# Kept rows of a routed FFN: gathered by index on GpSimd and turned on TensorE, in place of products with a choice matrix

## What is computed

```python
def ffn(x, w_r, b_r, w1, b1, w2, b2):        # x: attention's output, 64 x 64 x 512
    k = int(l * 0.5)                         # 32 of the 64 tokens of a sequence
    scores = jnp.einsum('bld,d->bl', x, w_r) + b_r
    _, idx = jax.lax.top_k(scores, k)
    x_sel = jnp.take_along_axis(x, idx[:, :, None], axis=1)
    h = jax.nn.gelu(jnp.einsum('bkd,df->bkf', x_sel, w1) + b1)
    out_sel = jnp.einsum('bkf,fd->bkd', h, w2) + b2
    return jnp.zeros_like(x).at[batch_ix, idx].set(out_sel)
```

## Time and profile before

| | |
|---|---|
| time, median of 3 runs | 2159.59 us (2158.35 to 2160.52) |
| the profiled execution: time, span | 2162.24 us, 2160.4 us |
| PE busy over the span | 1944.0 us, 90% |
| DVE, ACT, POOL busy | 72%, 56%, 55% |
| granted TensorE clock, mean | 0.966 |
| L1589 (products with `keep`) from 1300 to 1960 us | 23.2 us busy, x168 |

### The profile page before, as it was taken

One profiled execution on the slowest core, in us unless ns is written; L12 is line 12 of the kernel. 1 busy time (PEld: TensorE's weight loads), 2 busy tenths in 40 slices (PEclk: granted clock), 3 DMA queues, 4 the chain that ended last, 5 costly groups with the idle time before them and its releaser, 6 DMA issues.

```text
span 2160.4 us, 33041 instructions
## 1 busy us (share of the span) xinstructions
PE 1944.0 (90%) x9664; PEld 1344.5 (62%) x9664; DVE 1547.9 (72%) x2697; ACT 1199.8 (56%) x3210; POOL 1196.5 (55%) x1162
## 2 busy tenths in 40 slices
PE   5789998999899899978569999999999999999999
PEld 4666666676667666655246766757566575665755
DVE  6799999999999999999257654545545454554412
ACT  2666676666666666655246654645546454554512
POOL 1477887788877888777577763443443434340000
PEclk8899999999999999999879999999999999999999
DMA  4421332333323332230377443333233323331011
GB/s 141 168 110 66 129 118 90 115 129 129 121 83 121 129 120 107 88 113 30 101 208 246 134 115 96 83 102 104 80 109 93 102 76 96 95 85 37 14 52 47
DMA packets 149546, 225.83 MB, mean 105 GB/s; under 512 B 49859, under 2 KB 109254, under 8 KB 144002
## 3 DMA queue, kind: packets, MB, share of 16 engines
q1 hardware_dynamic: 116306, 161.94, 21.9%
q0 software_dynamic: 31744, 61.07, 10.1%
q10 hardware_dynamic: 1328, 0.91, 0.1%
HBM read 211.44 MB, written 40.51 MB: 117 GB/s over the span
## 4 chain that ended last, share of the span: by engine, by line
PE 43%; issue 2%; POOL 2%; DMA 2%; DVE 1%; ACT 1%; DVEq 0%; POOLq 0%; ACTq 0%
PE attn_psum L1610 11%; PE attn_psum L1624 10%; PE attn_psum L1576 5%; PE attn_psum L1562 4%; PE attn_psum L1549 4%; PE attn_psum L1542 4%; PE attn_psum L1533 2%; PE attn_psum L1640 2%; PE attn_psum L1589 1%; DMA kv<-in_kv_rows,old_now 1%; POOL kv L1214 1%; POOL kv L1206 1%; PE attn_psum L1523 1%; DMA kv<-kv_scratch,new_now 0%; ACT xh L1295 0%
## 5 line engine op out<-in xcount | busy, mean ns | idle before, releaser
L417 POOL TENSOR_TENSOR hid<-hid,bc 128x1024 f32<-128x1024 f32 x256 | 620.6, 2434 | 192.9 <-DVE hid L810 192.3
L938 PE MATMUL scan_psum<-hid,ident 128*128 128x256 f32 x2048 | 540.1, 394 | 108.9 <-POOL hid L417 108.9
L810 DVE TENSOR_TENSOR_SCAN hid<-scan_psum,dbu 128x1024 f32<-128x1024 f32 x256 | 581.7, 2273 | 4.7 <-ACT scan_psum L460 4.6
L938 PEld LDWEIGHTS scan_psum<-hid,ident 128*128 128x128 f32 x2048 | 383.9, 194 | 286.6 <-POOL hid L417 143.8
L460 ACT ACTIVATE scan_psum<-delta,neg_a 128x252 f32<-128x252 f32 x1024 | 423.9, 465 | 122.9 <-DVE hid L810 120.9
L1402 DVE CUSTOM_DVE_ANT_0 prob<-attn_psum,mask 128x336 f32<-128x336 f32 x256 | 120.6, 505 | 384.5 <-PE attn_psum L1542 383.0
L754 DVE TENSOR_TENSOR dbu<-scan_psum,bc 128x1024 f32<-128x1024 f32 x256 | 307.2, 1200 | 0.1
L1263 ACT COPY p_t<-attn_psum 112x384 f32<-112x384 f32 x256 | 121.5, 483 | 293.1 <-PE attn_psum L1549 292.8
L903 PE MATMUL scan_psum<-w_qkv,x 128*128 128x512 f32 x512 | 260.2, 594 | 3.9 <-ACT sq L520 2.4
L1624 PE MATMUL attn_psum<-w,ffn_hid 128*128 128x512 f32 x512 | 239.0, 596 | 8.9 <-DVE y_sb L1454 8.9
L1610 PE MATMUL attn_psum<-xs_in,w 128*128 128x256 f32 x1024 | 238.0, 387 | 0.6 <-ACT th L1296 0.5
(11 more groups left out here) (176 smaller groups left out, 2619.4 us busy)
## 6 DMA issues: line engine op xcount, KB each, us to landing
bc<-bc_scratch SPq DMA_DIRECT2D x32, 2048.0 KB, 7.3
q_scratch<-qg SPq DMA_DIRECT2D x32, 260.0 KB, 2.1
q_in<-q_scratch SPq DMA_DIRECT2D x32, 260.0 KB
x_pair<-in_x_pairs SPq DMA_DIRECT2D x32, 256.0 KB, 2.8
xt<-in_x_tp SPq DMA_DIRECT2D x16, 512.0 KB, 8.4
x_scratch<-x SPq DMA_DIRECT2D x16, 512.0 KB, 2.9
kv_scratch<-kvg SPq DMA_DIRECT2D x32, 256.0 KB, 2.0
w<-in_w SPq DMA_DIRECT2D x8, 1024.0 KB, 9.1
```

Source lines behind the costliest of these rows:

```text
L417: pool.tensor_tensor(hid[:, r, :, :], hid[:, r, :, :], bc[q // 2][:, 4 * j:4 * j + 4, 1, :], ALU.mult).then_inc(pool_hc, 1)
L810: nc.vector.tensor_tensor_scan(hid[:, k % RING, :, :].rearrange("p n t -> p (n t)"), decay[k % 2], dbu[:, k % RING, :, :].rearrange("p n t ...
L938: mm = nc.tensor.matmul(yc, ident[:], hid[:, k % RING, i, :], start=False, stop=(k % 4 == 3 and i == 3))
```

## The change

- **Rows by index.** `router_take`, `take_rows`, the store of `xs` and `load_xs` go. SP stores each pair's `a_sb` to memory as it is (`store_a`, 256 KB a pair). POOL gathers the 128 kept rows of two pairs with one indirect DMA (`gather_rows`) to `x_rows`, 128 by 512, PE turns them in four transposes (`turn_x`) into `a_bank`, and ACT copies them to `xs_in` (`take_x`): for tt = 0 in pair 4(t+1)+1 and for tt = 1 in pair 4(t+1)+2, both in w = 0. In the latter `ffn_first` stands two items later in PE's queue and waits for `take_x`.
- **Scores spread by a turn.** `router_row` is one transpose of the scores, each repeated along a row; `r_diag` goes.
- **Ranks spread by a turn.** `router_keep` is cut in two. `router_rank` (the counting) moves to the head of DVE's w = 3, before the two maxima. PE turns the ranks (`router_ranks`) in w = 3 between its two `turn_p`. `router_keep`, at its old place, waits for that and makes `keep_t` with one comparison, then the index list `r_idx` with two more instructions.
- **POOL's loop.** The second eight sequences are written out too, so the loop runs from 2. A gather of tile t's rows stands behind sequence 8(t+1)+5 for tt = 0 and behind sequence 8(t+2)+1 for tt = 1.

```diff
-            for s in range(NKV):
-                gather(0, s)
-            with pool.Fori(1, B // NKV) as i:
+            def gather_rows(t, tt):
+                wait(pool, dve_keep, 2 * (4 * t + 2 * tt + 2), pool_mark)
+                for h in range(2):
+                    wait(pool, st_a[h], 16 * (2 * t + tt + 1), pool_mark)
+                wait(pool, pe_xt, 2 * t + tt - 1, pool_mark)
+                pool.indirect_dma_start(x_rows[tt][:], None, S["a"][tt],
+                                        bass.IndirectOffsetOnAxis(ap=r_idx[tt][:, 0:1], axis=0)
+                                        ).then_inc(ld_xg[tt], 16)
+            def eight(i):
                 for s in range(NKV):
                     gather(i, s)
+                    if s == 5:
+                        gather_rows(i - 1, 0)
+                    if s == 1 and not (isinstance(i, int) and i == 1):
+                        gather_rows(i - 2, 1)
...
+            eight(1)
+            with pool.Fori(2, B // NKV) as i:
+                eight(i)
...
+            def take_x(t, tt):
+                act.wait_ge(pe_xt, 2 * t + tt + 1)
+                wait(act, pe_h, NH * t)
+                nc.scalar.copy(xs_in[:, :, P * tt:P * tt + P], a_bank.rearrange("p (c t) -> p c t", c=NCH)
+                               ).then_inc(act_xt, 1)
...
+            def router_keep(m, i, j):
+                h = j % 2
+                rows = slice(64 * h, 64 * h + 64)
+                dve.wait_ge(pe_rank, m + 1)
+                wait(dve, st_keep[h], 16 * (2 * i + j // 2))
+                v.scalar_tensor_tensor(keep_t[h][rows, :], a_bank[rows, P:2 * P], slot_no[rows, :], slot_own[rows, :],
+                                       ALU.is_equal, ALU.mult).then_inc(dve_keep, 1)
...
-                nc.tensor.matmul(a_bank[:, 0:P], ones[:], r_diag[:], start=True, stop=True).then_inc(pe_row, 1)
+                nc.tensor.transpose(a_bank[:, 0:P], r_s[:].to_broadcast([P, P]), ident[:]).then_inc(pe_row, 1)
-            def router_take(m, h):
-                pe.wait_ge(dve_keep, m + 1)
-                nc.tensor.matmul(a_bank[64 * h:64 * h + 64, P:2 * P], keep[:], ident[:], start=True, stop=True)
+            def router_ranks(m):
+                pe.wait_ge(dve_rank, m + 1)
+                nc.tensor.transpose(a_bank[:, P:2 * P], r_rank[:].to_broadcast([P, P]), ident[:]).then_inc(pe_rank, 1)
+            def turn_x(t, tt, m):
+                pe.wait_ge(ld_xg[tt], 16 * (t + 1))
+                wait(pe, act_xt, 2 * t + tt)
+                wait(pe, dve_keep, 2 * min(m - 1, NG) if isinstance(m, int) else 2 * (m - 1))
                 for c in range(NCH):
-                    mm = nc.tensor.matmul(a_bank[:, 2 * P + 2 * SEL * c:2 * P + 2 * SEL * c + 2 * SEL],
-                                          a_sb[:, P * c:P * c + P], keep[:], start=True, stop=True)
-                mm.then_inc(pe_xs, 1)
+                    mm = nc.tensor.transpose(a_bank[:, P * c:P * c + P], x_rows[tt][:, P * c:P * c + P], ident[:])
+                mm.then_inc(pe_xt, 1)
...
-                    pe.wait_ge(ld_xs, 16 * (t + 1))
+                    pe.wait_ge(act_xt, 2 * (t + 1))
...
-                    if w == 0 and parts.prev2:
-                        router_take(m - 2, h)
+                    if w == 0 and parts.first and j in (1, 2):
+                        turn_x(i - 1, j - 1, m)
...
+                    if w == 3 and parts.prev:
+                        router_ranks(m - 1)
```

More of the change, by code:

```diff
@@ L1009, in attention_ffn_block @@
         r_s = sb("r_s", [P, 1])
-        r_diag = sb("r_diag", [P, P])
+        r_tok = sb("r_tok", [P, 1])
+        r_idx = [sb(f"r_idx{i}", [P, 1], I32) for i in range(2)]
         r_own, r_gt, r_eq, r_rank = (sb(n, [P, 1]) for n in ("r_own", "r_gt", "r_eq", "r_rank"))
-        keep = sb("keep", [P, 2 * SEL])
         keep_t = [sb(f"keep_t{i}", [P, P]) for i in range(2)]
-        xs = [sb(f"xs{i}", [P, NCH, 2 * SEL]) for i in range(2)]
+        x_rows = [sb(f"x_rows{i}", [P, D]) for i in range(2)]
         w1, w2 = W["w1"], W["w2"]
@@ L1167, in pair @@
                 if parts.prev2:
-                    store_rows(m - 2, 2 * i + j // 2 - 1, h)
-                if parts.first and j == 1:
-                    load_xs(i - 1)
+                    store_keep(m - 2, 2 * i + j // 2 - 1, h)
+                if parts.prev:
+                    store_a(m - 1, i if j else i - 1, (j - 1) % 4)
                 if parts.second and j < 2:
@@ L1573, in project @@
                 pe.wait_ge(act_o, m + 1)
-                wait(pe, act_xs, 2 * m)
+                wait(pe, dve_keep, 2 * m)
+                if turned is not None:
+                    pe.wait_ge(act_xt, turned)
                 for c in range(4):
@@ L1704, in program @@
     S["keep"] = nc.dram_tensor("keep_scratch", [NG, 2 * SEL, P], F32).ap()
[L1705 to L1706 removed]
+    S["a"] = [nc.dram_tensor(f"a_scratch{i}", [2 * P, D], F32).ap() for i in range(2)]
     with ExitStack() as ctx:
```

103 lines of the change are left out of this document (55 added, 48 removed).

## The result

The changed kernel takes 2201.3 us (median of 5 runs, 2193.39 to 2204.69), the kernel before 2160.52 beside it (2158.35 to 2163.7): ratio 1.0185, 95% interval 1.017 to 1.0199. It is slower by 41 us where 4.8 were forecast. Its profiled execution took 2193.39 us (span 2191.6) and was its fastest; its other four show a lower mean clock (0.949 to 0.953 against 0.957) with their longer spans.

The account below looks back on a forecast made before the run. PE was taken to bound the kernel from pair 6 on. Start wait 17.1, clock 2.5, slots -28.6 and DVE wait 13.4, plus 0.4, gave +4.8 us: 2164.4 against the median 2159.59, range 2152 to 2177.

Parts of the forecast that it names:

- The start wait: First FFN product, pair 6: waits for tile 0's second row gather in POOL's queue, starting at 1224.7 not 1207.56, +17.1 us.
- The bound of 23: Upper end, in us, of the start-wait term, if POOL's written-out sequences are no faster than its loop.
- The clock behind it: After PE's idle time in pair 6: granted clock falls, costing 2.5 us, ends 1.7 and 3.4.
- The saved slots: PE from pair 6 on: choice and score products go, turns come, -28.6 us.
- The wait of DVE: DVE waits for PE's turned ranks, so everything behind the maxima is 0.57 us late: +13.4 us, ends 5 and 20.
- Place (1): A tile's second pair: PE's wait for take_y grows from 1.36 to 1.95 us, six times, +3.5; pair 33 adds 1.1.
- R: Start of PE's rank turn, near the end of each pair; the forecast counts DVE's chain of instructions from it.
- Place (2): A tile's third pair: PE waits 1.3 us for take_x behind ACT's two exponentials, six times, 7.8; pair 34 adds 0.9.
- Place (3): A tile's last pair and the next tile's first: a GELU product stands between, so PE waits only 0 to 0.1 us.
- rival D: Clock falls at the new PE waits of some 2.0 us, twelve falls of 2.2 each: 2191 us; chance 0.08.
- 0.4 added for rounding: Added to the summed terms, +4.4 us, for place (3) and for issue costs that rows round away, giving +4.8.
- A: The terms hold as summed: 2164.4 us, ends 2158 to 2172; chance 0.64.

## Why the prediction was wrong

It had the sign and rivals that name most of what happened, and a time 37 us too low: outside its range. Term by term, against the two profiled executions:

**The start wait: right in mechanism and place, 3.9 short.** Forecast 1224.7 for the first FFN product, found 1228.55, +21.0. The step that failed is that eight written-out sequences would go at the 8.0 us of four earlier ones. POOL opens sequence 8 at 1136.05 and sequence 16 at 1206.07, with one gather of rows in between, so 8.6 each. Six of the eight took 7.9 to 8.4, but sequence 8 took 11.5, since one issue in it stood for 3.41 us for a landing. Rows 4 had a sign of this: sequences 6 and 7, written out as well, took from 1118.37 to 1136.27, 8.95 each, with a stand of 2.14 for a landing. What holds such landings up no run shows. The first row is of the kernel before, the two behind it are of the changed kernel:

```profile
1124.72 0.98 POOL L1214 DMA_INDIRECT kv<-kv_scratch,new_now  x1 [2.14 <-DMA kv<-in_kv_rows,old_now]
...
1143.97 0.99 POOL L1216 DMA_INDIRECT kv<-kv_scratch,new_now  x1 [3.41 <-DMA kv<-in_kv_rows,old_now]
...
1223.38 0.96 POOL L1234 DMA_INDIRECT x_rows<-a_scratch,r_idx  x1 [0.30 <-issue]
```

The bound of 23 was for this case. The rest of the term (two loop sequences, 3.4 us from issue to PE, 1.8 from the turns to the product) came out to 0.5 us each. The clock behind it cost 0.9 us in the first FFN product (4.38 in place of 3.45) and not 2.5.

**The saved slots: 21.6, not 28.6.** The mis-sized pieces are partly visible. The scores' turn takes 0.20 where 0.125 was put, the ranks' turn 0.11, and the choice's products gave back some 1.16 and not 1.25: the values' slot ahead of them was 0.71 with them (1461.72 to 1462.43) and is 0.80 now. That makes 24 to 25; some 3 us of the gap are in no row that I can point to. The 275 ns for one turn, from Part 4 of the Trainium skill's page "TensorE: Matmul & The Clock Gate", would by an estimate have left some 12 us of saving; slots of 0.11 to 0.20 don't bear it out as a price, though 0.27 is the length that the rows record for one.

**The wait of DVE: 24.1 and not 13.4.** Place (1), `y_sb`: +6.6 us against 4.6. The chain has the forecast's steps, each a little longer. These rows are of DVE in the changed kernel, R being 1443.83:

```profile
1444.27 0.36 DVE L1465 SCALAR_TENSOR_TENSOR keep_t<-attn_psum,slot_no,slot_own 64x128 f32<-64x128 f32 x1 [3.51 <-PE attn_psum L1628]
...
1445.27 0.16 DVE L1431 RECIPROCAL share<-total 128x1 f32<-128x1 f32 x1
...
1446.39 0.51 DVE L1426 CUSTOM_DVE_ANT_0 prob<-attn_psum,mask 128x336 f32<-128x336 f32 x1
```

R + 0.44, 1.44 and 2.56 stand where R + 0.3, 1.15 and 2.15 were forecast: the maxima are 0.41 later still, and 1.95 becomes 2.36. The durations of the instructions had been added, and not the distances between their starts. Place (2), `xs_in`: +7.7 against 8.7, the wait 1.33 against 1.3, but in four tiles and not six (0.84 in two). Place (3), from a tile's last pair to the next: this is the step that failed, and the largest miss. "0 to 0.1" was found to be 9.9 over three places. The 0.1 held for a DVE that goes on at once. At these places, where its loop turns, it stands for 2.4 to 2.6 us first, and the row of it was in the trace of before: an idle time of an engine that was not late, and therefore free, until the change made it late. The second stand, of 1.5 to 1.7 us before the maxima, is not in the trace of before and could not be read from it.

**The clock: rival D, given 0.08.** The forecast took the clock as unmoved by waits near 2.0, and rival D gave each fall 2.2 us. Waits of 2.1 to 2.7 do bring falls, eight of nine in the changed kernel, of 1.7 us each and twice of 3.4; but so do some of the waits of 1.7 to 1.8 that the kernel before has. In sum 41.4 us of low clock against 26.2 cost 7.6 us in the profiled pair. D's 2191 us lies near the profiled 2193 by luck: it had 26 us of clock and none of the 9.9. The changed kernel's other executions have a mean clock 0.004 to 0.008 lower over 2200 us, which is 9 to 18 us of work and covers the 8 by which their median lies above the profiled one.

The sum of the misses: 3.9 at the start, 7.0 slots, 10.7 waits, 5.1 clock (7.6 against the 2.5 put behind the start), less 0.4 added for rounding: 26.3, the distance between the 4.8 forecast and the 31.2 found to 0.1. The other 10 us up to the 41 of the medians are that the profiled execution of the changed kernel was 8 us under its median and that of the kernel before 2 above. A and D weren't alternatives: the waits that A priced were the ones at which D began.

## What to carry to other kernels

When a step becomes a wait of an engine with a fixed queue, price the place of the instruction that releases it, too: one line moved in front of a long product was worth 37 us here, on a chip where the kernel before takes 2160 us. An idle stretch without a releaser (a loop's turn) is a price that is paid as soon as the engine comes late to it, so it belongs in the sum of every change that delays that engine. And a gather that is put behind others on a busy queue costs what is ahead of it; move it up, and look at what it then delays.

## What was not expected of the hardware

- At a turn of its loop DVE stood for 2.24 to 2.43 us in the kernel before and 2.40 to 2.62 in the changed one, there with 1.52 to 1.72 more before the maxima; ACT stood for 0.96 to 1.11, and PE 1.71 in the one row that shows it.
- TensorE's clock fell behind eight of nine waits of 2.1 to 2.7 us, and behind a wait of 1.7 in some tiles and traces and not in others; a fall cost 1.7 us of work, at times 3.4. With one kind of wait filled there were as many falls, behind another.
- The way from the end of a matmul to DVE and the distances from one short DVE instruction to the next added 0.41 us to a chain of 2.15.
- Two chips ran the same kernel before in 2284 and 2287 us in place of 2160. Their traces, which are of other versions, show idle stretches of ACT and DVE of up to 17 and 19 us, and on one of them the changed kernel was faster than the kernel before.
